# Softmax attention on one core: three shared PSUM banks for weighings and side products, and reciprocals of the row sums alone, laid out by DMA

## The reference: what is computed

```python
a = jax.nn.softmax(jnp.einsum('bhsd,bhtd->bhst', q, k) * D ** (-0.5), axis=-1)
if causal:                                    # a mask after the softmax: s > t is kept
    a = a * mask
o = jnp.einsum('bhst,bhtd->bhsd', a, v)       # per head; then the heads are joined and projected
```

## Time and profile before

| | us |
|---|---|
| median of 3 runs | 4577.88 (4573.99 to 4580.83) |
| the profiled execution | 4581.35 |
| its span, first to last instruction | 4580.1 |
| mixed attention, from 240 to 1513 us of the span | 1273 |
| a1, from 1890 to 2510 us | 620 |
| a2, from 2780 to 3826 us | 1046 |

### The profile page before, as it was taken

The page is one execution under the profiler, slowest core; times in us unless marked ns, Lnnn a source line. Parts: engine busy times, 40 slices in busy tenths (PEclk is TensorE's granted clock), DMA queues, the critical chain, the costliest instruction groups (busy, mean ns, idle before and its releaser), DMA issues. The chain is left out here.

```text
span 4580.1 us, 50086 instructions
## 1 busy us (share of the span) xinstructions
PE 3762.4 (82%) x18124; PEld 2022.6 (44%) x18124; DVE 2487.1 (54%) x4355; ACT 1618.6 (35%) x2977; POOL 961.8 (21%) x1026
## 2 busy tenths in 40 slices
PE   7588899899998784676777638999999996789998
PEld 4333333333332571333333534444444443657777
DVE  6547566576574245443534647766666662533332
ACT  1024545545455220132223203454545553122222
POOL 1100000000000011131222322454554554200000
PEclk9858978988877796687888867999999998889999
DMA  0111111202110311331341014333333321022121
GB/s 33 39 39 33 49 25 30 50 23 52 25 29 7 112 47 40 58 45 23 47 54 37 30 44 67 55 49 55 53 55 48 53 37 57 4 95 65 57 68 55
DMA packets 114349, 211.13 MB, mean 46 GB/s; under 512 B 19124, under 2 KB 69176, under 8 KB 111032
## 3 DMA queue, kind: packets, MB, share of 16 engines
q1 hardware_dynamic: 114104, 207.94, 21.9%
HBM read 82.74 MB, written 8.39 MB: 20 GB/s over the span
## 5 line engine op out<-in xcount | busy, mean ns | idle before, releaser
L883 DVE TENSOR_REDUCE a_mp<-bank 128x1 f32<-128x384 f32 (+2 forms) x1280 | 699.0, 590 | 409.7 <-PE bank L742 401.0
L848 ACT ACTIVATE a_p<-bank 128x512 f32<-128x512 f32 (+1 forms) x1088 | 591.0, 596 | 635.6 <-PE bank L767 625.9
L883 DVE TENSOR_REDUCE mx_mp<-bank 128x2 f32<-128x768 f32 (+4 forms) x640 | 595.5, 951 | 317.0 <-PE bank L742 222.4
L848 ACT ACTIVATE mx_p<-bank 128x512 f32<-128x512 f32 (+3 forms) x1088 | 549.2, 557 | 512.8 <-PE bank L767 333.2
L919 POOL TENSOR_TENSOR a_pair<-a_p 128x512 f32<-128x512 f32 x384 | 481.5, 1278 | 524.9 <-ACT a_p L848 524.7
L742 PE MATMUL bank<-a_ks,a_qs 96*128 96x384 f32 (+2 forms) x1280 | 463.6, 434 | 125.0 <-issue 105.0
L767 PE MATMUL bank<-a_qs,a_ks 98*128 98x512 f32 (+1 forms) x1088 | 437.4, 476 | 65.6 <-DMA a_qs<-a_mt 51.6
L742 PEld LDWEIGHTS bank<-a_ks,a_qs 96*128 96x128 f32 x1280 | 261.5, 207 | 418.5 <-issue 290.5
L767 PE MATMUL bank<-mx_qs,mx_ks 50*128 50x512 f32 (+3 forms) x1088 | 368.6, 526 | 64.3 <-ACT mx_p L848 49.2
L199 POOL TENSOR_TENSOR rs<-ve,neghalf 128x4 f32<-128x4 f32 (+2 forms) x80 | 75.3, 941 | 1341.4 <-DVE ve L194 1340.9
L742 PE MATMUL bank<-mx_ks,mx_qs 48*128 48x384 f32 (+4 forms) x1280 | 312.9, 448 | 31.3 <-DVE mx_mp L883 22.9
(11 more groups left out here) (301 smaller groups left out, 5711.4 us busy)
## 6 DMA issues: line engine op xcount, KB each, us to landing
sf_raw<-in_h_w SPq DMA_DIRECT2D x64, 512.0 KB, 3.5
a_ks<-a_kh SPq DMA_DIRECT2D x96, 192.0 KB, 4.5
ex_w<-in_L_ffn_w SPq DMA_DIRECT2D x16, 1024.0 KB, 4.9
a_qs<-a_qh SPq DMA_DIRECT2D x64, 256.0 KB, 6.6
mx_ks<-mx_kh SPq DMA_DIRECT2D x192, 48.0 KB, 2.1
a_ks<-a_kl SPq DMA_DIRECT2D x48, 192.0 KB, 5.2
mx_qs<-mx_qh SPq DMA_DIRECT2D x128, 64.0 KB, 2.2
a_qs<-a_ql SPq DMA_DIRECT2D x32, 256.0 KB, 5.7
```

The lines of the kernel that those rows point to most:

```text
L848: act.activation(probs[place % 8][0:kp, q0:T], self.bank(part, n, kb, h)[0:kp, q0:T], ACT.Exp, scale=scale).then_inc(*self.frees(part, n, ...
L883: v.tensor_reduce(best[:, tiled * j:tiled * j + tiled, i, ci], bank[:, 0:w] if tiled == 1 else bank[:, :, 0:w], AX.X, ALU.max).then_inc(*s ...
```

## The change

Four things:

1. The `misc` bank joins `b_banks`: one ring of three banks that weighings and side products take in turn.
2. At the end of a job the reciprocals are taken of the sums alone. SP lays the four sum rows (4 x 512 values) over all 128 partitions, 16 values each ("gather", into `thin`); VectorE takes one reciprocal of 128x16; SP writes it to a small DRAM tensor ("flat") and reads it back with four DMAs, each of which lays one head's row over 32 partitions of `rec` ("spread"). The matmul, its 0/1 matrix and the copy of the spread sums are gone. `raw` has two buffers.
3. These steps come two halves apart (one in a1), the quotient 13 halves after the last block's end instead of 8 (9 in a1).
4. The schedule: the projections ("finish") come later by two or three blocks, some value products of a2 earlier, `lead` is 4 instead of 3 in the mixed attention, and within a half the splits go ahead of other steps. `bias_twice` reads one row twice instead of two equal rows.

```diff
 def split(now):
-                for step in list(due[at]):
+                for step in sorted(due[at], key=lambda step: step[0] not in ("split", "tops_turned")):
 def beside_half():
-            if half < free_at or any(step[0] in ("weights", "spread", "turn_tops") for step in steps):
+            if half < free_at or any(step[0] in ("weights", "turn_tops") for step in steps):
 # the end of a job, if kb == last:
                         due[half + 3].append(("result", n))
-                        due[half + 4].append(("totals" if job.summed else "spread", n))
-                        for i in range(TB):
-                            due[half + 5 + i].append(("inverse", n, i))
-                        due[half + 4 + TB].append(("quotient", n))
+                        if job.summed:
+                            due[half + 4].append(("totals", n))
+                        for i, step in enumerate(("gather", "inverse", "flat", "spread", "quotient")):
+                            due[half + 5 + i * (1 if job.summed and last < TB else 2)].append((step, n))
 # softmax_attention
-        raw, rec = sb("raw", [P, T]), sb("rec", [P, T])
+        raws, rec, thin = [sb(f"raw{i}", [P, T]) for i in range(2)], sb("rec", [P, T]), sb("thin", [P, HG * T // P])
+        flat = nc.dram_tensor(f"{tag}_flat", (2, HG, T), F32, kind="Internal").ap()
-        b_banks = Ring(self.banks[3:5] if tiled == 1 else self.banks[4:6])
+        b_banks = self.spare = Ring([*(self.banks[3:5] if tiled == 1 else self.banks[4:6]), self.banks[7]])
-        misc = self.misc = Ring(self.banks[7:8])
-        self.wide = Ring(b_banks.slots + misc.slots)
 # q, k and turn_tops: self.take(misc, ...) becomes self.take(b_banks, ...)
 # pe_part
-            elif part == "spread":
-                bank = self.take(misc, "spread", n)
-                pe.wait_ge(*self.empty("spread", n))
-                pe.wait_ge(*self.freed("num", n))
-                pe.matmul(bank[:, :], spread[:, :], raw[:, :], start=True, stop=True).then_inc(*self.fills("spread", n))
 # act_part
             elif part == "result":
+                if n >= 2:
+                    act.wait_ge(*has("y_made", n - 2))
+                act.wait_ge(*has("values_summed", n, blocks(n) - 1))
+                act.activation(raws[n % 2][:, :], self.bank("num", n)[:, :], ACT.Copy).then_inc(*self.frees("num", n))
+            elif part == "totals":
                 if n:
                     act.wait_ge(*has("y_made", n - 1))
-                act.wait_ge(*has("values_summed", n, blocks(n) - 1))
-                act.activation(raw[:, :], self.bank("num", n)[:, :], ACT.Copy).then_inc(*self.frees("num", n))
-            elif part == "totals":
                 act.wait_ge(*has("weights_summed", n, blocks(n) - 1))
                 act.activation(rec[:, :], self.bank("den", n)[:, :], ACT.Copy).then_inc(*self.frees("den", n))
-            elif part == "spread":
-                act.wait_ge(*self.full("spread", n))
-                act.activation(rec[:, :], self.bank("spread", n)[:, :], ACT.Copy).then_inc(*self.frees("spread", n))
 # dve_part
             elif part == "inverse":
-                i, = at
-                cs = slice(P * i, P * i + P)
-                v.wait_ge(*self.freed("den" if summed else "spread", n))
-                v.reciprocal(rec[:, cs], rec[:, cs]).then_inc(*up("inverse_made", n))
+                if n:
+                    v.wait_ge(*has("flat_landed", n - 1))
+                v.wait_ge(*has("thin_landed", n))
+                v.reciprocal(thin[:, :], thin[:, :]).then_inc(*up("inverse_made", n))
 # pool_part, quotient
-                g.wait_ge(*has("inverse_made", n))
+                g.wait_ge(*has("spread_landed", n))
+                raw = raws[n % 2]
 # sp_part
+            elif part == "gather":
+                if n:
+                    sp.wait_ge(*has("flat_landed", n - 1))
+                sp.wait_ge(*self.freed("den" if summed else "num", n))
+                sums_in = rec[0:P:P // HG, :] if summed else raws[n % 2][D:P:P // HG, :]
+                sp.dma_start(thin[:, :], sums_in).then_inc(*self.lands("thin_landed", n))
+            elif part == "flat":
+                sp.wait_ge(*has("inverse_made", n))
+                if n >= 2:
+                    sp.wait_ge(*has("spread_landed", n - 2))
+                sp.dma_start(flat[n % 2].rearrange("h (q t) -> (h q) t", t=HG * T // P), thin[:, :]
+                             ).then_inc(*self.lands("flat_landed", n))
+            elif part == "spread":
+                sp.wait_ge(*has("flat_landed", n))
+                if n:
+                    sp.wait_ge(*has("y_made", n - 1))
+                for h in range(HG):
+                    sp.dma_start(rec[32 * h:32 * h + 32, :], flat[n % 2][h:h + 1, :].to_broadcast([32, T])
+                                 ).then_inc(*self.lands("spread_landed", n))
 # mixed_attention: schedule of finish, and lead
-                    beside[begin + 5 + i].append([("finish", b - 1, 1 + i)])
-                at_once[begin + 11].append([("finish", b - 1, TB + 1)])
-                at_once[begin + 14].append([("finish", b - 1, TB + 2)])
+                    beside[begin + 7 + i].append([("finish", b - 1, 1 + i)])
+                at_once[begin + 13].append([("finish", b - 1, TB + 1)])
+                at_once[begin + 16].append([("finish", b - 1, TB + 2)])
-            beside, at_once, [[("finish", NB - 1, i)] for i in range(TB + 3)], 2.6, 3)
+            beside, at_once, [[("finish", NB - 1, i)] for i in range(TB + 3)], 2.6, 4)
 # block_attention, a2
-                    lay(b, 0, *finish_of(b - 1, 2, 4, 5, 6, 7))
-                lay(b, 0, *values_of(b, 1, 8, 9, 10, 11))
+                    lay(b, 0, *finish_of(b - 1, 2, 7, 8, 9, 10))
+                lay(b, 0, *values_of(b, 1, 2, 3, 4, 5))
 # block_attention, a1
-                    lay(b, 0, *finish_of(b - 1, 1, 3, 4, 5, 6))
+                    lay(b, 0, *finish_of(b - 1, 1, 6, 7, 8, 9))
```

More of the change, by code:

```diff
@@ L59 @@
 ATTENTION = ("stack", "split", "peak", "tops", "turn_tops", "tops_turned", "weigh", "values", "weights", "pair",
-             "result", "spread", "totals", "inverse", "quotient")
+             "result", "totals", "gather", "inverse", "flat", "spread", "quotient")
 Job = namedtuple("Job", "b g cuts first sub mask pairs summed nk add y vw q qb k kb q_after k_after values values_after y_after needs")
@@ L553, in peaks @@
             while found < min(to, len(flow)) and most:
-                _, n, ci, j, i = flow[found]
+                _, n, ci, *_ = flow[found]
                 while now and (n, ci) not in stacked:
@@ L579, in beside_half @@
                     yield step
-        self.spare = self.wide
         for group in before:
             yield from side(group)
-        self.spare = self.misc
         while found < total[0]:
@@ L693, in softmax_attention @@
         if not summed:
-            spread = sb("spread", [P, P])
-            g.memset(spread[:, :], 0.0).then_inc(*up("mask_made"))
-            g.wait_ge(*has("mask_made"))
-            sv = spread[:, :].rearrange("p (g r) -> p g r", g=HG)
-            g.affine_select(out=sv, in_=sv, compare_op=ALU.not_equal, fill=1.0, base=-D,
-                            pattern=[[-P // HG, HG], [0, P // HG]], channel_multiplier=1).then_inc(*up("mask_made"))
-            pe.wait_ge(*has("mask_made"))
             tile = self.take(n_banks, "num_cleared")
@@ L721, in pe_part @@
                         pe.wait_ge(*event)
-                    bank = self.take(misc, "q", n)
+                    bank = self.take(b_banks, "q", n)
                     pe.wait_ge(*self.empty("q", n))
@@ L728, in pe_part @@
                         pe.wait_ge(*event)
-                    bank = self.take(misc, "k", n, ci)
+                    bank = self.take(b_banks, "k", n, ci)
                     pe.wait_ge(*self.empty("k", n, ci))
@@ L748, in pe_part @@
             elif part == "turn_tops":
-                bank = self.take(misc, part, n)
+                bank = self.take(b_banks, part, n)
                 pe.wait_ge(*self.empty(part, n))
@@ L1001, in mixed_attention @@
         wp = self.weight(scope, "weights_landed", "L0_xattn_Wp", [P, NG, C])
-        row = self.rows(scope, ["L0_xattn_bv", "L0_xattn_bcv", "L0_xattn_bcv", "L0_xattn_bp"], "mx")
-        bias_twice = self.row_tile[:, 1:3, :].rearrange("p n c -> p (n c)")
+        row = self.rows(scope, ["L0_xattn_bv", "L0_xattn_bcv", "L0_xattn_bp"], "mx")
+        bias_twice = self.row_tile[:, 1:2, :].to_broadcast([P, 2, C])
         xts = [sb(f"xt{i}", [P, KC, T]) for i in range(2)]
@@ L1107, in dve_part @@
                 v.tensor_tensor(vcs[b % 2][0:kp, t:t + n, :, 0:D], spread(self.bank("context_v", b, i - 1)[0:kp, 0:n * C]),
-                                spread(bias_twice[0:kp, 0:n * C]), ALU.add).then_inc(*self.frees("context_v", b, i - 1))
```

(1 more changed line is left out.)

## The result

The changed kernel takes 4602.85 us (median of 4 runs, 4596.81 to 4611.83) against 4577.75 in the same comparison: ratio 1.0057, 95% interval 1.0039 to 1.0075. The profiled execution took 4603.73 us with a span of 4602.5. Over the span TensorE is busy for 3727.1 us (3762.4 before), VectorE for 2303.6 (2487.1), ScalarE for 1589.0 (1618.6), at a mean granted clock of 0.849 (0.861).

A forecast was written before the change was run, and what follows sets the result against it. TensorE's instruction stream was taken to set the time. Terms of -70 - 20 - 50 - 20 - 20 + 8 + 32 + 18 = -122 us took 4581.35 to 4459, less 3.5: 4456 us, range 4355 to 4600.

The forecast's parts named there:

- The side product in the ring: Weighings in the shared ring wait for VectorE to free a side product's bank: 18 us, set to 0, range 0 to 140.
- Three banks for the weighings: A third bank cuts the weighings' waits for ScalarE: -70 us in the mixed attention, -20 in a1 and a2.
- The spread matmul: Its 64 instructions leave TensorE's stream in the mixed attention: -50 us, between 35 and 67.
- the reciprocals: Smaller reciprocals on VectorE shorten TensorE's waits for it: -20 us in the mixed attention, -20 in a1 and a2.
- the DMAs: End of each job by three DMA round trips: +8 us in the mixed attention, +32 in a1 and a2.
- the ends of stages: Uncovered chain from last copy to quotient, 10.4 us each at the three stages' ends: +18 us.
- Schedule: Later projections, earlier value products and lead 4 move work within the same stream: 0 us.
- Slower: Rival, chance 0.17: DMAs in loaded queues, waited for in order in a1 and a2; at 6 us per job 4616 us.
- Hidden: Rival, chance 0.17: the weighings' wait was cover, ScalarE or VectorE is next late; 4539 us.
- The clock: Rival, chance 0.12: fewer waits raise the mixed attention's granted clock from 0.81 to 0.90, 69 us more, 4387 us.
- Nothing: Rival, chance 0.06: the DMAs give the gain back in equal part; within 9 us of 4578.
- What would show it: Signs for: ScalarE wait under 150 us, mixed attention about 1140; against: weighings waiting for ql, kl or a turned maximum.

The follow-up runs named there:

- free_first: The changed kernel, its three shared banks given out by earliest-laid release instead of in strict turn: 4436.53 us, ratio 0.9687.
- early_split: The changed kernel with its strict ring, the split put right behind its stack instead of a half later: 4422.89 us, ratio 0.9634.
- ff_unsorted: free_first without the precedence of splits within a half: 4396.17 us, ratio 0.9578.
- own_bank: The changed kernel, but side products have bank 7 to themselves again and the weighings a ring of two: 4529.62 us, ratio 0.9882.
- ff_only: The kernel before, with free-first sharing of the three banks and nothing else: 4479.60 us, ratio 0.9765.
- own_unsorted: own_bank without the precedence of splits and turned maxima within a half: 4501.35 us, ratio 0.9812.
- own_a1_engines: own_bank, with a1's reciprocals on VectorE as before and the quotient at 8 halves there: 4511.20 us, ratio 0.9831.
- ring_old_recip: The changed kernel, ring and schedule kept, but the end of a job as before (spread matmul, full reciprocals, no DMAs): 4653.08 us, ratio 1.0151.
- old_places: The changed kernel with lead 3, a2's value products in their old places and no precedence of splits: 4629.60 us, ratio 1.0111.
- own_three_weigh: own_bank, but in a1 and a2 the weighings have three banks and the peaks two: 4613.07 us, ratio 1.0055.
- ring_only: The kernel before with the strict ring of three banks and nothing else: 4678.82 us, ratio 1.0204.

## Why the prediction was wrong, point by point

*The step that failed* is "The side product in the ring": "I take 0.05 each, 18 us, since two halves of some 2.3 us ... lie between". It lies in the order that the generator writes. A side product is taken at the end of half h; half h + 1 takes the other two banks; the first weighing of half h + 2 needs the side product's. But the split is laid at the end of half h + 1, behind the peaks of that half. Between the release and its waiter lie no halves at all. The term, 0 in the sum with 140 as its upper bound, measured 176 us against free_first by stage (85, 15 and 76) and 178 against early_split: above even the bound. The bound came from the waits of the spread matmul (0.4 us each), a user whose turn isn't fixed to the second half after a side product. With the release early or the turn free the time comes near the forecast of 4456: early_split took 4423 us and free_first 4437. That it comes so near is in part luck, since the precedence of splits, put at 0, costs 40 us of it (ff_unsorted: 4396).

*Three banks for the weighings.* -70 in the mixed attention; own_bank to free_first gives -76, and before to ff_only, without the rest of the change, -99.5. -20 in a1 and a2; they give -9 and -5, and -5 and -6, each about what repeats or less. The working from one block gave the right size (100 us before the share of the side products was taken off), and the choice near the lower bound for a1 and a2 held.

*The spread matmul, the reciprocals, the DMAs, the ends of stages*: -50 - 40 + 8 + 32 + 18 = -32 forecast; own_bank against before is 1.2% or 54 us. In the mixed attention -50 - 20 + 8 = -62 stood against -60 measured, in a1 and a2 together -20 + 32 = +12 against +10 and -18. The reciprocal took 0.25 us (0.23 estimated). These sums agree, but the terms in them are not shown one by one: own_bank has the new schedule too, and its precedence of splits costs 11 us in the mixed attention (own_unsorted); with free-first sharing the same parts give 36 us there (1164.2 in ff_only, 1127.9 in free_first). In a1 the net of DMAs against reciprocals on VectorE was a cost of 14 us in own_a1_engines, 29 in ring_old_recip and 7 without the precedence; the sum had 16 for the DMAs less a1's share of the 20 for the reciprocals. In a2 the one pair that tells, ring_old_recip against the changed kernel, has 5 us, which says nothing. The chain at a stage's end was 7.2 and 7.1 us where 10.4 stood. Some 2 of the 3.2 us are a slip in the sum: it added the issue (0.65 us, three times) to the landing, but the landing is counted from the start of the issue, as the flat write shows, which reached its waiter 1.43 us after its issue began and 1.09 after it ended, while the shortest landing in its row is 1.4. The rest is that these DMAs landed in less than the 2.1 us of a 48 KB one. The Trainium skill (DMA: Bandwidth & Descriptors, Anatomy of one DMA) says that the write receipt is most of a DMA's fixed time and is heaviest at HBM; its section describes DMAs issued by GpSimd, and these are SP's. These rows don't bear out a heavier one at HBM: the flat write reached its waiter in 1.43 us, the gather within SBUF in 1.98. The 2 us more per job that the prediction made of it were its own estimate, and nothing of that size is there.

*Schedule*: taken at 0. The precedence of splits costs 28 us by whole medians with their own bank and 40 with free-first sharing. In the strict ring it costs 19 us in a1, and elsewhere no gain of it is shown: old_places has about the same mixed attention without it (there the old `lead` differs too), and its share in the 21 us of a2 isn't told apart from that of the value products. It moves a split within its half; what was needed was another half.

*The rivals.* "Slower" came, but not by its mechanism: with the DMAs and without the ring it is faster (own_bank), without the DMAs and with the ring slower (ring_old_recip). VectorE did wait 155.2 and 68.6 us for `thin`, of which 45.05 and 49.49 are the ends of a2 and of the mixed attention, where VectorE had nothing to do for most of that time. The other 110 and 19 us are not what made the kernel slower: in own_bank, which is faster than the kernel before, the two rows are 157.3 and 106.0. GpSimd stood 1082.9 us before the spread DMAs in the mixed attention, and TensorE behind them once, for 12.3 us. "Hidden" is half right for a1 and a2 (free_first, own_three_weigh), not for the mixed attention, where free sharing gave 76 to 99.5 us. "The clock": in the mixed attention it fell from 0.81 to 0.79, and it was 0.83 to 0.85 in the versions in which the waits went. "Nothing" doesn't hold: the ratio's interval excludes 1.

*What would show it*: the ScalarE wait of under 150 us came (108.2), but the mixed attention of some 1140 us that was to come with it didn't (1213); and "weighings that wait for ql, kl or a turned maximum" was named as what would prove the forecast wrong, and did. The place was seen, its price was not worked out: that would have needed one walk through three halves of the order.

## The hardware

The granted clock follows the waits, and somewhat more is won by it than the working of the clock rival had it (0.3 of the half-clock time that goes; here 65 of 164 us, 0.4). ring_only and ff_only have the same 5602 matmuls in the mixed attention and the same work on VectorE and ScalarE. The clock is 0.80 in the one and 0.85 in the other; TensorE's busy time is 1111.8 and 1047.0 us. Of the 119 us between the stages, 65 are thus busy time of the same matmuls, and only 54 are idle time. At 0.80, 40% of 1283 us (513) are at 1.2 GHz, at 0.85 30% of 1164 (349). If work at 1.2 GHz takes twice as long, the 164 us that went are worth 82 us of time, of which TensorE is busy for 0.88: 72 us by this estimate, against 65 measured. This pair agrees, with 0.80 in the stage that waits more and 0.85 in the other. Waits are not all of it: free_first has a shorter stage than ff_only and 0.83. In this pair the stage became shorter by 2.2 times the idle time that went (119 for 54), from the changed kernel to early_split by 2.4 times (91 for 39), and in a2, at 0.96 to 0.98, by 1.5 times (76 for 51, with 25 of busy time, 969.7 to 944.4).

Not expected either: the 8 KB write to DRAM (mx_flat) landed in 1.6 us by the median, and the 8 KB DMA from SBUF to SBUF reached its waiter in 1.98 and 1.95 us at the two stage ends, later than the write (1.43 and 1.42). The waiters differ (VectorE, SP), and so does the layout, so the reason stays open.

## What to carry to other kernels

Before two kinds of user share a ring of banks in strict turn, walk through the order and find for each taking how many steps lie between the last release laid down and the waiter on it; a holder that another engine frees late costs every user behind it, and here that was some 180 of 4600 us. Then either lay the release at once (one moved step gave this back) or let users take the bank that is released first. When a wait vanishes from one row of the profile, look for the engine that now stands in its place before counting it as gained.
